# Graph layer with 16 relations: later places for the key chain, and every third tile through stage one in two fp32r parts

## The chip, the cores and the metric

One core of a Trainium2 chip runs the whole program. The metric is the device time of the execution in microseconds (us); less is better. The engines are named as the profile names them: PE is TensorE (its matmuls; PEld its weight loads), DVE is VectorE, ACT is ScalarE, POOL is GpSimd, SP is SyncE.

## The reference, cut to what matters

```python
# h: 6250 x 256, weight: 16 x 256 x 256, 206250 edges sorted by dst
transformed = einsum('ni,rio->rno', h, weight)
msg = transformed[rel_type, src] * norm          # per edge
out = segment_sum(msg, dst, num_segments=6250)   # per node
x = layernorm(x + out)
```

All of it is float32. Each edge takes the source node's row, scales it by the edge's weight `norm`, multiplies it with its relation's matrix and adds it to the row of its destination node.

## The kernel before, in words

The kernel turns the order round: it first sums the scaled source rows for each pair (node, relation) and multiplies with the matrices afterwards.

The 6250 nodes are cut into NB = 49 blocks of 128 nodes. Since the edges are sorted by destination, the edges of a block are a stretch of the edge list; the kernel takes CT = 35 tiles of 128 edges for each block, and tile t can only hit a window `WIN[t]` of the block's nodes. With 16 relations a window is 64 to 304 columns wide (column = node x 16 + relation).

**Stage one** of tile t is a matmul that scatters 128 edges: the stationary operand is the tile's gathered rows (128 edges x 128 features, for each of two feature halves h), the moving operand is `spread`, a 128-edge by window matrix that holds the edge's `norm` in the column of its key and zero elsewhere. DVE makes `spread` by comparing a column index with the edge's key and multiplying by norm (L605). The result accumulates in PSUM (`ps_a`) in four groups of 32 nodes (GROUPS = 4), two of which are open at a time (OPEN = 2); ten of the tiles touch two groups. Each float32 matmul of the program is two matmul instructions with two weight loads in the trace, so a tile in one group is four pairs (2 halves x 2), one in two groups is eight. Groups end with tiles 9, 17, 26 and 34.

A finished group is taken out of PSUM in two fp32r parts: ACT writes the upper part `a_hi` (L678), DVE the rest `a_lo` (L581). **Stage two**, one block behind, is 32 products (L766 with 512 columns, L768 with 256), all fp32r; they are dealt out over the 35 tiles of the next block's stage one, one or two after each tile from tile 4 on (`products_after`). A block's last group is taken out during tiles 3 and 4 of the next block.

**The gathers**: POOL fetches the 128 source rows of each tile with one indirect DMA (L433) into a ring of 35 slots (`rows`, ROWS = 35). Before tiles 0, 5, 10, ... it waits until PE has summed the tiles whose slots come free (`wait(pool, tiles_summed, b, CT, t + BATCH - ROWS)`). The last two tiles of a block (OPTIONAL) are only gathered when they hold edges of the block.

**The key chain** of block b + 1 runs beside the tiles of block b. Its steps stand at fixed places of the hand-written order of each engine, by the tuple PREPARE. Step 0 (ACT, tile 1) converts the loaded edge arrays `raw` to float (`convert_edges`, L658). Step 1 (PE, tile 2) transposes them into `ps_m` (`turn_edges`, L750). Step 2 (ACT, tile 4) copies them to `meta` (`copy_edges`, L666). Step 3 (DVE, tile 6) makes the indices `idx` and the keys (`keys`, L528 to L547) and signals `keys_made`, for which POOL waits before it gathers tile 0 of block b + 1. Step 4 (PE, tile 8) sums the hits of the optional tiles (`sum_hits`, L736). Step 5 (DVE, tile 12) casts that sum for POOL (`convert_hits`, L552). Block 0 has its own tuple, PREPARE_0, which is 19 more at every place.

Every engine goes through its own program in order. DVE makes `spread` at most RING = 10 tiles ahead of PE: the wait for `tiles_summed` in front of each. ACT has nothing in stage one but the evacuations, the key chain and a square root for the layer norm.

## Time and profile before

| | |
|---|---|
| median of 3 runs | 2565.3 us (2549.6 to 2580.5) |
| the profiled execution's own time | 2584.87 us |
| its span | 2583.2 us |
| mean granted TensorE clock | 0.926 |
| PE busy / POOL busy / DVE busy / ACT busy | 86% / 60% / 45% / 10% |

The profiled execution is 19.6 us above the median of the three runs. PE is the busiest engine, but its busy time is made of modelled ends of pipelined matmuls; the spacing of starts is what tells a matmul's cost. A block takes some 51 us.

### The profile page before, as it was taken

To read this page: it belongs to the slowest core of one execution; us is meant where nothing else is said; L and a number is where in the kernel's file an instruction comes from. 1 tells how busy PE (TensorE), PEld (TensorE's weight loads), DVE (VectorE), ACT (ScalarE), POOL (GpSimd) and SP (SyncE) were. 2 spreads that over 40 slices of the span, in tenths; PEclk is the share of its full clock that TensorE was granted. 3 is DMA by queue.
4 is the path that set the end of the run, shared out by engine and by line. 5 is a ranking of instruction groups with operands and counts; after the bars stand their busy time and mean duration, and the time that the engine had idled before them with its cause. 6 is when DMAs were issued, how large, how long until landed. Compare 5 with 4: busy or idle time off the path is not lost.

```text
span 2583.2 us, 33166 instructions
## 1 busy us (share of the span) xinstructions
PE 2219.3 (86%) x12267; PEld 1956.2 (76%) x12267; DVE 1151.6 (45%) x2871; ACT 271.2 (10%) x559; POOL 1560.6 (60%) x1675
## 2 busy tenths in 40 slices
PE   5589889889988998888888888888898888888888
PEld 4477777778777777777777778777787777777777
DVE  4344444344444443544444345444544444444443
ACT  2011101101111010101110011011101100110100
POOL 5666666656665666666666566666666666666660
PEclk8799999989998999999989998998999999999998
DMA  4333333333333333333333333333333333333331
GB/s 134 101 94 95 94 94 93 94 90 90 93 95 90 94 93 93 94 92 94 93 99 92 91 91 97 91 91 95 96 94 93 96 90 93 93 94 94 89 92 17
DMA packets 107084, 238.86 MB, mean 92 GB/s; under 512 B 30580, under 2 KB 54176, under 8 KB 106926
## 3 DMA queue, kind: packets, MB, share of 16 engines
q0 software_dynamic: 79056, 215.91, 29.5%
q1 hardware_dynamic: 27870, 20.81, 2.8%
q8 instruction: 103, 1.69, 0.3%
q14 instruction: 55, 0.45, 0.1%
HBM read 230.13 MB, written 6.62 MB: 92 GB/s over the span
## 4 chain that ended last, share of the span: by engine, by line
PE 77%; another core or an unknown queue 8%; issue 7%; DVE 4%; ACT 2%; SPq 0%; DMA 0%; DVEq 0%
PE ps_a L799 55%; PE ps_z L766 14%; PE ps_z L768 7%; DVE a_lo L581 2%; ACT a_hi L678 2%; DVE spread L605 1%; DMA w_raw<-in_L_gnn_weight 0%; PE ps_m L750 0%; SPq L344 0%; ACT meta L666 0%; PE ps_m L736 0%; DVE key L533 0%; DVE key_hit L542 0%; DVE hits L545 0%
## 5 line engine op out<-in xcount | busy, mean ns | idle before, releaser
L433 POOL DMA_INDIRECT rows<-in_x,idx x1646 | 1557.0, 946 | 958.5 <-issue 441.4
L799 PE MATMUL ps_a<-spread,rows 128*128 128x128 f32 (+15 forms) x8820 | 1817.3, 339 | 305.4 <-issue 174.3
L799 PEld LDWEIGHTS ps_a<-spread,rows 128*128 128x128 f32 x8820 | 1394.0, 201 | 481.4 <-issue 219.2
L766 PE MATMUL ps_z<-w_parts,a_hi 128*128 128x512 f32 x1568 | 875.3, 560 | 29.8 <-DVE a_lo L581 25.0
L605 DVE TENSOR_SCALAR spread<-ps_i,key,meta 128x272 f32<-128x272 f32 (+13 forms) x1715 | 750.7, 502 | 50.4 <-remote 29.7
L581 DVE TENSOR_TENSOR a_lo<-ps_a,a_hi 128x512 fp32r<-128x512 f32 x392 | 252.4, 686 | 1055.3 <-ACT a_hi L678 990.7
L768 PE MATMUL ps_z<-w_parts,a_lo 128*128 128x256 f32 x1568 | 453.9, 289 | 7.7 <-issue 7.7
L678 ACT ACTIVATE a_hi<-ps_a 128x512 fp32r<-128x512 f32 x392 | 212.8, 595 | 1848.9 <-PE ps_a L799 1483.5
L766 PEld LDWEIGHTS ps_z<-w_parts,a_hi 128*128 128x128 f32 x1568 | 317.1, 202 | 64.8 <-DVE a_lo L581 28.0
L768 PEld LDWEIGHTS ps_z<-w_parts,a_lo 128*128 128x128 f32 x1568 | 316.8, 202 | 37.6 <-issue 13.5
L528 DVE CAST idx<-meta 128x35 int32<-128x35 f32 x50 | 10.4, 208 | 120.7 <-ACT meta L666 117.2
L552 DVE CAST late_hits<-ps_m 1x2 int32<-1x2 f32 x49 | 7.1, 146 | 112.7 <-remote 106.1
L706 ACT ACTIVATE z_std<-z_mv,eps_col 128x1 f32<-128x1 f32 x49 | 14.4, 294 | 271.8 <-issue 204.7
L666 ACT ACTIVATE meta<-ps_m 128x140 f32<-128x140 f32 x50 | 14.6, 291 | 141.9 <-remote 138.6
L750 PE MATMUL ps_m<-ident,raw_f 35*128 35x35 f32 x150 | 18.9, 233 | 8.9 <-issue 4.8
L658 ACT ACTIVATE raw_f<-raw 35x384 f32<-35x384 int32 x50 | 25.7, 514 | 1.4 <-DMA raw<-in_edge_weight 1.4
L750 PEld LDWEIGHTS ps_m<-ident,raw_f 35*128 35x128 f32 x150 | 13.3, 139 | 16.5 <-issue 10.8
L560 DVE TENSOR_TENSOR z_own<-xr,ps_z 128x256 f32<-128x256 f32 x49 | 20.1, 411 | 9.0 <-PE ps_z L768 9.0
L564 DVE BATCH_NORM_STATS2 z_stat<-z 128x6 f32<-128x256 f32 x49 | 21.0, 428 | 1.7
L562 DVE TENSOR_TENSOR z<-z_own,ps_z 128x256 f32<-128x256 f32 x49 | 20.6, 421 | 1.7
L572 DVE TENSOR_SCALAR z_out<-z,z_mv,z_rstd 128x256 f32<-128x256 f32 x49 | 20.3, 415 | 1.8
L594 DVE TENSOR_TENSOR w_parts<-w_raw,w_parts 128x512 fp32r<-128x512 f32 x16 | 11.0, 689 | 22.2 <-issue 14.4
(52 smaller groups left out, 132.0 us busy)
## 6 DMA issues: line engine op xcount, KB each, us to landing
rows<-in_x,idx POOLq DMA_INDIRECT x1646
xr<-in_x SPq DMA_DIRECT2D x48, 128.0 KB
out<-z_out SPq DMA_DIRECT2D x48, 128.0 KB
w_raw<-in_L_gnn_weight SPq DMA_DIRECT2D x16, 256.0 KB
raw<-in_src SPq DMA_DIRECT2D x48, 17.5 KB
raw<-in_dst SPq DMA_DIRECT2D x48, 17.5 KB
raw<-in_edge_type SPq DMA_DIRECT2D x48, 17.5 KB
raw<-in_edge_weight SPq DMA_DIRECT2D x48, 17.5 KB
```

The lines of the kernel that those rows point to most:

```text
L433: pool.indirect_dma_start(rows[:, rows_slot(b, t), :], None, x, bass.IndirectOffsetOnAxis(ap=idx[:, b % 2, t:t + 1], axis=0)).then_inc(row ...
L562: dve.tensor_tensor(z[:, :], z_own[:, :], ps_z[:, b % 2, F:2 * F], ALU.add).then_inc(residual_added, 1)
L564: dve.bn_stats(z_stat[:, :], z[:, :]).then_inc(variance_steps, 1)
L572: dve.tensor_scalar(z_out[:, :], z[:, :], z_mv[:, 0:1], z_rstd[:, :], ALU.subtract, ALU.mult).then_inc(rows_normalised, 1)
L581: dve.tensor_tensor(a_lo[:, b % 2, h, :, at_g], ps_a[:, g % OPEN, h, :].rearrange("p (n r) -> p r n", r=R), a_hi[:, b % 2, h, :, at_g].bit ...
L605: dve.tensor_scalar(spread[:, slot, 0:(end - first) * R], iota[:, 0:(end - first) * R], key[:, b % 2, t:t + 1], meta[:, b % 2, 3, t:t + 1] ...
L658: act.activation(raw_f[:, :, :], raw[:, 0:3, :], ACT.Copy).then_inc(edges_converted, 1)
L678: act.activation(a_hi[:, b % 2, h, :, g * GN:(g + 1) * GN], ps_a[:, g % OPEN, h, :].rearrange("p (n r) -> p r n", r=R), ACT.Copy).then_inc ...
L750: ins = pe.transpose(ps_m[:, a * CT:(a + 1) * CT], v, ident[0:CT, 0:CT])
L766: pe.matmul(zk, a_hi[:, ak, h, r, :], w_parts[:, r, h, :, :].rearrange("p a f -> p (a f)"), start=n == 0, stop=False, skip_group_check=True)
L768: ins = pe.matmul(zk[:, 0:F], a_lo[:, ak, h, r, :], w_parts[:, r, h, 0, :], start=False, stop=n == KH * R - 1, skip_group_check=True)
L799: ins = pe.matmul(ps_a[:, g % OPEN, h, (begin - g * GN) * R:(stop - g * GN) * R], rows[:, rows_slot(b, t), h * P:(h + 1) * P], spread[:, s ...
```

## The change

It has two parts. First, three places of PREPARE move: the key chain on DVE from tile 6 to 16, the hit sum on PE from 8 to 20, the hit cast on DVE from 12 to 31. PREPARE_0 keeps its values, now written out. Second, the tiles t with t % 3 == 1 (1, 4, 7, ..., 34: twelve of 35) take another way through stage one. ACT multiplies the gathered rows by norm and rounds them to fp32r (`hi`); DVE makes a plain 0/1 matrix in fp32r (`onehot`) and the rest `lo` = rows x norm - hi; PE multiplies hi and lo, one after the other, with the same onehot, as fp32r matmuls into the same sums. The new tiles have four slots (HALVES). RING goes from 10 to 7.

```diff
-    RING = 10
+    RING = 7
+    HALVES = 4
-    PREPARE = (1, 2, 4, 6, 8, 12)
-    PREPARE_0 = tuple(t + 19 for t in PREPARE)
+    PREPARE = (1, 2, 4, 16, 20, 31)
+    PREPARE_0 = (20, 21, 23, 25, 27, 31)
+    SPLIT = tuple(t for t in range(CT) if t % 3 == 1)
+    NS = len(SPLIT)
+        def half_free(eng, b, t):
+            n = SPLIT.index(t)
+            if n >= HALVES:
+                wait(eng, tiles_summed, b, CT, SPLIT[n - HALVES] + 1)
+            else:
+                wait(eng, tiles_summed, b, CT, SPLIT[n - HALVES + NS] + 1 - CT)
 # DVE, each tile
-                        wait(dve, tiles_summed, b, CT, t + 1 - RING)
-                        dve.tensor_scalar(spread[:, slot, ...], iota[...], key[...], meta[...], is_equal, mult)
+                        if t in SPLIT:
+                            half_free(dve, b, t)
+                            dve.tensor_scalar(onehot[:, slot, 0:width], iota[:, 0:width], key[:, b % 2, t:t + 1],
+                                              None, ALU.is_equal).then_inc(split_parts_made, 1)
+                            wait(dve, upper_made, b, NS, SPLIT.index(t) + 1)
+                            dve.scalar_tensor_tensor(out=lo[:, slot, :], in0=rows[:, rows_slot(b, t), :],
+                                                     scalar=meta[:, b % 2, 3, t:t + 1],
+                                                     in1=hi[:, slot, :].bitcast(F32), op0=ALU.mult,
+                                                     op1=ALU.subtract).then_inc(split_parts_made, 1)
+                        else:
+                            (as before, with RING = 7)
 # ACT, each tile, behind the key chain's steps and ahead of the evacuations
+                        if t in SPLIT:
+                            (wait for the gathered rows of t)
+                            half_free(act, b, t)
+                            act.activation(hi[:, half_slot(t), :], rows[:, rows_slot(b, t), :], ACT.Copy,
+                                           scale=meta[:, b % 2, 3, t:t + 1]).then_inc(upper_made, 1)
 # PE, each tile
+                        if split:
+                            wait(pe, split_parts_made, b, 2 * NS, 2 * SPLIT.index(t) + 2)
+                            parts, cols = (hi[:, half_slot(t), :], lo[:, half_slot(t), :]), onehot[...]
...
-                            for g in groups:
-                                ins = pe.matmul(ps_a[...], rows[..., h * P:(h + 1) * P], spread[...], ...)
+                            for m, part in enumerate(parts):
+                                for g in groups:
+                                    ins = pe.matmul(ps_a[...], part[:, h * P:(h + 1) * P], cols[...], ...)
```

The waits of `copy_edges` count the split tiles apart from the others; nothing else changes.

## Rows read from the trace of the kernel before

**Rows 1.** The page: busy time by engine, and the chain that ended last.

```profile
PE 2219.3 (86%) x12267; PEld 1956.2 (76%) x12267; DVE 1151.6 (45%) x2871; ACT 271.2 (10%) x559; POOL 1560.6 (60%) x1675
...
PE 77%; another core or an unknown queue 8%; issue 7%; DVE 4%; ACT 2%; SPq 0%; DMA 0%; DVEq 0%
```

**Rows 2.** Waits: who waited for whom, us in total, times, longest.

```profile
PE ps_a L799 <- issue: 174.3, 238, 10.6
...
PE ps_a L799 <- DVE spread L605: 126.8, 43, 6.1
DVE idx L528 <- ACT meta L666: 117.2, 22, 6.6
...
POOL rows L433 <- DVEq L536: 75.3, 22, 11.3
```

**Rows 3.** Timeline of all engines: two steps of the key chain and what follows.

```profile
306.92 0.37 PE L750 MATMUL ps_m<-ident,raw_f 35*128 35x35 f32 x3
...
312.83 0.29 ACT L666 ACTIVATE meta<-ps_m 128x140 f32<-128x140 f32 x1 [6.01 <-remote]
...
315.14 0.96 PE L799 MATMUL ps_a<-spread,rows 128*128 128x176 f32 x4 [4.37 <-DVE spread L605]
...
1342.82 0.19 PE L736 MATMUL ps_m<-key_hit,ones 128*1 128x2 f32 x2
...
1349.27 0.15 DVE L552 CAST late_hits<-ps_m 1x2 int32<-1x2 f32 x1 [4.53 <-remote]
```

**Rows 4.** Timeline of POOL, the first and last of ten gathers, then the next.

```profile
1364.68 0.94 POOL L433 DMA_INDIRECT rows<-in_x,idx  x1 [1.49 <-PE ps_a L799]
...
1375.92 0.95 POOL L433 DMA_INDIRECT rows<-in_x,idx  x1 [0.30 <-issue]
1379.53 0.94 POOL L433 DMA_INDIRECT rows<-in_x,idx  x1 [2.66 <-PE ps_a L799]
```

**Rows 5.** Timeline of POOL, the first and last of 25 gathers, then the next.

```profile
64.08 0.94 POOL L433 DMA_INDIRECT rows<-in_x,idx  x1 [11.32 <-DVEq L536]
...
94.08 0.95 POOL L433 DMA_INDIRECT rows<-in_x,idx  x1 [0.30 <-issue]
99.38 0.94 POOL L433 DMA_INDIRECT rows<-in_x,idx  x1 [4.36 <-remote]
```

**Rows 6.** Windows: busy time, clock, DMA share, GB/s in two stretches.

```profile
74.00:100.00 26.00, 6.04 (x29) 4.91 (x29) 4.12 (x11) 0.00 (x0) 16.69 (x18) 0.62 0.35 97
1350.00:1400.00 50.00, 43.14 (x240) 38.27 (x239) 23.30 (x59) 4.93 (x11) 31.97 (x34) 0.90 0.31 90
```

**Rows 7.** Timeline of PE, 1325 to 1332 us: start, us, operation.

```profile
1325.31 1.19 PE L799 MATMUL ps_a<-spread,rows 128*128 128x304 f32 x4
...
1326.68 1.19 PE L799 MATMUL ps_a<-spread,rows 128*128 128x304 f32 x4
...
1329.21 0.81 PE L799 MATMUL ps_a<-spread,rows 128*128 128x192 f32 x4
...
1330.21 0.61 PE L799 MATMUL ps_a<-spread,rows 128*128 128x128 f32 x4
...
1331.00 0.55 PE L799 MATMUL ps_a<-spread,rows 128*128 128x64 f32 x4
```

**Rows 8.** Groups by line, weight loads: busy, mean ns of one, idle before.

```profile
L799 PEld LDWEIGHTS ps_a<-spread,rows 128*128 128x128 f32 x8820 | 1394.0, 201 | 481.4 <-issue 219.2 <-DVE spread L605 144.0
L766 PEld LDWEIGHTS ps_z<-w_parts,a_hi 128*128 128x128 f32 x1568 | 317.1, 202 | 64.8 <-DVE a_lo L581 28.0 <-issue 8.7
```

**Rows 9.** Groups by line, shapes apart: the nearest operations to the added ones.

```profile
L678 ACT ACTIVATE a_hi<-ps_a 128x512 fp32r<-128x512 f32 x392 | 212.8, 595 | 1848.9 <-PE ps_a L799 1483.5 <-remote 250.2 <-issue 115.2
...
L562 DVE TENSOR_TENSOR z<-z_own,ps_z 128x256 f32<-128x256 f32 x49 | 20.6, 421 | 1.7
```

**Rows 10.** Timeline of DVE in one block: the keys, and tile 15's spread.

```profile
1338.10 0.23 DVE L528 CAST idx<-meta 128x35 int32<-128x35 f32 x1
...
1351.83 1.41 DVE L605 TENSOR_SCALAR spread<-ps_i,key,meta 128x240 f32<-128x240 f32 x3
```

More of the change, by code:

```diff
@@ L114, in build @@
     OPTIONAL = (CT - 2, CT - 1)
+    SPLIT = tuple(t for t in range(CT) if t % 3 == 1)
+    NS = len(SPLIT)
+    assert NS % HALVES == 0 and CT % ROWS == 0
     CONFIRM = 3
@@ L189, in build @@
         rows = sb("rows", [P, ROWS, F])
+        hi = sb("hi", [P, HALVES, F], F32R)
+        lo = sb("lo", [P, HALVES, F], F32R)
+        onehot = sb("onehot", [P, HALVES, WMAX], F32R)
         spread = sb("spread", [P, RING, WMAX])
@@ L602, in tile_block @@
                         first, end = WIN[t]
-                        wait(dve, tiles_summed, b, CT, t + 1 - RING)
-                        dve.tensor_scalar(spread[:, slot, 0:(end - first) * R], iota[:, 0:(end - first) * R],
-                                          key[:, b % 2, t:t + 1], meta[:, b % 2, 3, t:t + 1],
-                                          ALU.is_equal, ALU.mult).then_inc(spreads_made, 1)
+                        width = (end - first) * R
+                        if t in SPLIT:
+                            half_free(dve, b, t)
+                            slot = half_slot(t)
+                            dve.tensor_scalar(onehot[:, slot, 0:width], iota[:, 0:width], key[:, b % 2, t:t + 1],
[6 more added lines that the diff above has]
+                        else:
+                            wait(dve, tiles_summed, b, CT, t + 1 - RING)
+                            dve.tensor_scalar(spread[:, ring_slot(b, t), 0:width], iota[:, 0:width],
+                                              key[:, b % 2, t:t + 1], meta[:, b % 2, 3, t:t + 1],
+                                              ALU.is_equal, ALU.mult).then_inc(spreads_made, 1)
                     for g in range(GROUPS):
@@ L783, in tile_block @@
                             seek_turn()
-                        wait(pe, spreads_made, b, CT, t + 1)
-                        if t in OPTIONAL:
-                            wait(pe, optional_rows_in, b, 1, 1)
-                        else:
-                            wait(pe, rows_in[t], b, 16, 16)
+                        split = t in SPLIT
+                        if split:
+                            wait(pe, split_parts_made, b, 2 * NS, 2 * SPLIT.index(t) + 2)
+                            parts, cols = (hi[:, half_slot(t), :], lo[:, half_slot(t), :]), onehot[:, half_slot(t), :]
+                        else:
+                            wait(pe, spreads_made, b, CT - NS, sum(n not in SPLIT for n in range(t + 1)))
+                            if t in OPTIONAL:
+                                wait(pe, optional_rows_in, b, 1, 1)
+                            else:
+                                wait(pe, rows_in[t], b, 16, 16)
+                            parts, cols = (rows[:, rows_slot(b, t), :],), spread[:, ring_slot(b, t), :]
                         first, end = WIN[t]
@@ L796, in tile_block @@
                                     wait(pe, a_lower_made, b, GROUPS * KH, KH * (g - OPEN) + h + 1)
-                            for g in groups:
-                                begin, stop = max(first, g * GN), min(end, (g + 1) * GN)
-                                ins = pe.matmul(
-                                    ps_a[:, g % OPEN, h, (begin - g * GN) * R:(stop - g * GN) * R],
-                                    rows[:, rows_slot(b, t), h * P:(h + 1) * P],
-                                    spread[:, slot, (begin - first) * R:(stop - first) * R],
-                                    start=group_tiles[g][0] == t, stop=False, skip_group_check=True)
+                            for m, part in enumerate(parts):
+                                for g in groups:
+                                    begin, stop = max(first, g * GN), min(end, (g + 1) * GN)
+                                    ins = pe.matmul(
+                                        ps_a[:, g % OPEN, h, (begin - g * GN) * R:(stop - g * GN) * R],
+                                        part[:, h * P:(h + 1) * P],
+                                        cols[:, (begin - first) * R:(stop - first) * R],
+                                        start=group_tiles[g][0] == t and m == 0, stop=False, skip_group_check=True)
                         ins.then_inc(tiles_summed, 1)
```

15 lines of the change are left out of this document (12 added, 3 removed).

## The prediction, made before the changed kernel was run

> **What bounds the kernel now.** I read the page first: its chain that ended last is 77% PE, and PE is busy 86% of the span [rows 1]. Busy time alone would say that less matmul work is less time. The waits correct that: besides its work PE loses 174.3 us with nothing that the profile can name and 126.8 us waiting for DVE's spreads, DVE waits 117.2 us in its key step for ACT's meta, and POOL waits 75.3 us for the keys [rows 2]. So I looked at the places where this happens. PE's transposes of the next block start at 306.92 and take 0.37 us, but ACT, which waits for nothing else, copies their result only at 312.83; DVE has to wait with its keys, and PE with the next spread, until 315.14 after an idle 4.37 us. In another block the hit sum starts at 1342.82 and DVE casts it at 1349.27, 6.5 us later [rows 3]. The signal of a matmul that is long done comes 5 to 6 us late.
>
> When it is late can be read on POOL. A gather starts every 1.25 us ((94.08 - 64.08) / 24 [rows 5]) while nothing stops it. At 1364.68 POOL begins ten in a row, the last at 1375.92, and then sits 2.66 us until PE's slots are reported free at 1379.53 [rows 4]. The late signals lie inside such unbroken runs, and come through some two microseconds after the run ends. Ten is the longest run of the steady state. The warm-up has one of 25, from 64.08 to 94.08, and POOL goes on at 99.38 [rows 5]. In its stretch from 74 to 100 us PE is busy 6.04 us of 26, at a mean granted clock of 0.62; in an ordinary stretch it is busy 43.14 of 50, at 0.90 [rows 6]. So a long run does to PE what a short one does not: PE can work ahead of its own late signals for a few tiles, no more. I take as this kernel's second bound that the gathers must come in runs of at most about ten. They need 33 to 35 x 1.25 = 41 to 44 us of a block's 51 us, and the 7 to 10 us that are left are the pauses that let PE's signals through.
>
> **Split tiles, PE.** Two neighbouring tiles of 304 columns start 1.37 us apart, a tile of 192 and its successor 1.00 us [rows 7]; both stretches hold four matmuls and one product. The difference over 4 x 112 columns is 0.83 ns a column, two cycles at 2.4 GHz, and what is left, 0.36 us, is the product: 512 + 256 fp32r columns at 0.47 ns, so about one cycle a column at 512 and 256. The tiles of 128 and 64 columns are 0.79 us apart, which makes 0.11 us a matmul at either width, a floor [rows 7]. The split keeps the number of matmuls (four a group) and takes one cycle a column in place of two. Per tile, 4 x (0.83 x width ns, at least 110) less 4 x (0.42 x width, at least 110): nothing for tiles 1, 16 and 34, 0.10 for tile 4, 0.04 for 7, 0.31 for 10, 0.36 each for 13 and 31, 0.41 for 19, 0.45 for 22, 0.20 for 25, 0.51 for 28. That is 2.75 us a block, 49 blocks: -135 us. No fp32r matmul under 256 columns is in this trace. The bounds: one cycle there too (the nearest rows, of the same type), or no better than float32's four cycles over its two matmuls, which paid twice by hi and lo is +4.1 us a block, +200 us. I take one cycle, the rate of the type's own rows; the split at 256 and more alone gives 1.37 us a block.
>
> The Trainium skill ("TensorE: Matmul & The Clock Gate", Weight-path perf modes) says that weight loads go up to four times as fast when the type is not FP32. If fp32r counted as another type, the floor would fall for the parts and the saving would rise to an estimated 5.0 us a block. The trace has the weight loads of both types at 201 and 202 ns [rows 8], so I leave it a small chance.
>
> **Split tiles, the other engines.** DVE's onehot has the shape of the spread that it replaces: nothing. `lo` is new: 12 times, as DVE's 128x256 two-operand add, 421 ns [rows 9], 5 us a block on an engine that is busy 45%. `hi` on ACT is half the elements of the evacuation's 595 ns [rows 9], between 0.3 and 0.6 us, 12 times, 4 to 7 us on an engine busy 10%. Both are beside PE's work. But the order matters: `hi` of tile 4 stands on ACT behind the meta copy, which waits for PE's transposes of tile 2. Before, only the key chain waited there; now `hi`, `lo`, and PE's tile 4 do. With a prompt signal that is 0.3 + 0.45 + 0.42 us of chain against 1.1 us of PE's tiles 2 and 3, next to nothing; with a late one it is the whole 5.9 us [rows 3]. I take 1.5 us a block, bounds 0 and 5.7: +70 us. RING 7 leaves DVE seven tiles ahead, 7 x 1.2 us = 8 us, more than a late signal: nothing, at most 1 us a block where the tiles are short.
>
> **The key chain's places.** DVE no longer waits for meta at tile 6. That returns at most the 126.8 us that PE waited for spreads [rows 2]; I take -100. The hit sum at 20 and the cast at 31 carry two small operations and a wait each; POOL needs the cast only before its tile 33, after the block's end. Nothing.
>
> What the key step also moves is the gathers. POOL may not gather tile 0 of the next block before `keys_made`. In one block the keys start at 1338.10; the place ahead of tile 16 is right after tile 15's spread, at 1351.83 + 0.5 [rows 10]. So the next block's gathers start 14 us later, while PE is in its tile 11 or 12. Today POOL stands at its slot limit nearly always, and each batch of five is let through by PE's next five tiles: that makes the pauses. After the change POOL is idle from the end of one block's gathers (42 us after they began) to the next keys, some 9 us at one stretch: all of the slack in one place, in which nothing is held up. When it starts, PE has done 11 tiles, so ten gathers are free at once; the batches at 10 and 15 need 15 and 20 tiles, and PE has them, since its signals are late only from about the fifth gather on, at tile 15 or 16. The first run is then 15 to 20 long. Price: in the run of 25 PE did 6.04 us of work in the 26 us that followed its first eight gathers [rows 6], so about 1 to 1.25 us are lost for each gather beyond ten. I take 15: +6.25 us a block, bounds 0 (the gate shuts at ten as now) and 12.5 (a run of 20). The keys move for 47 blocks (block 0 keeps its places): +294 us.
>
> The clock follows the stalls: 0.90 in the ordinary stretch, 0.62 in the starved one [rows 6]. If the mean goes from 0.926 to 0.88, the 37 us of PE work in a block take 2 us more: +94 us, bounds 0 and 190.
>
> **The sum** is -135 + 70 - 100 + 294 + 94 = +223 us on the profiled execution's own 2585, 2808. The median of the runs is 20 us lower: **2790 us**. With the bounds of the run's length and of the clock it goes from 2650 to 2950.
>
> **The rivals.**
> - The longer run does no harm, or does not come about: POOL is stopped at ten by the late signals themselves, as now. For it speaks that it is a feedback (a slower PE closes the gate sooner), and that both long runs of the trace are in the warm-up, where PE lacked products and keys too. Against it, PE has ample work in the stretch of rows 6. Then the split's 135 us and a part of the key wait remain: 2565 - 135 = 2430, from 2380 to 2480 by what of the 100 the wait at tile 4 takes back.
> - Narrow fp32r matmuls cost as much as float32's or twice that: this ends on the slow side without any gathers. It decides where a part is under 256 columns, in twelve of the fifteen tile-and-group pairs. With the forecast's gathers 2790 + 67 = 2857 up to 2790 + 334 = 3124; with harmless gathers up to 2765.
> - Gains and losses cancel: a run only two gathers longer (+2.5 us a block) eats the split and the key wait: 2540 to 2590.
> - The weight loads of the parts are faster, by the skill's rule above: the saving is 5.0 in place of 2.75 us a block, 110 us less, 2680 with the forecast's gathers. The rows speak against it.
>
> **How the numbers follow.** Forecast 0.45, harmless gathers 0.26, narrow parts dear 0.17, cancelling 0.09, faster weight loads 0.03. Faster by over 1% is the second alone, 0.26; within 1% (about what a measurement of this kernel tells from no change) the fourth, 0.09; slower the rest, 0.65. The forecast's own range is 2650 to 2950. The range that should hold the time 8 times in 10 has to take in the fast side: 2425 to 2960 leaves out half of the second case and of the third, some 0.17.
>
> **What the profile of the changed kernel would show.** Right: gathers in runs of 15 and more once a block, after a wait for the keys of some 9 us; PE idle with no named cause growing from 174 us to several hundred; the granted clock under 0.90; DVE's wait for meta gone from the keys, and PE waiting for `lo` of tile 4. Wrong: runs of ten at most, and a block under 50 us. The rates can be read from the starts of tiles 28 (304 columns) and 31 (240): 0.87 and 0.80 us to the next tile for one cycle a column, if tile 31 takes 1.16 us it is no faster than before, and with 1.96 us it is twice as dear. What would make the whole wrong is the reading that the runs cause the late signals: if it is the other way round, POOL's pause being the effect of a signal that is late for another reason, then the place of the keys costs nothing.

## The result, and the profile after

| | before | after |
|---|---|---|
| median | 2567.7 us (4 runs) | 3028.9 us (4 runs, 3006.5 to 3033.8) |
| the profiled execution's own time | 2584.87 us | 3029.99 us |
| mean granted TensorE clock | 0.926 | 0.809 |

The ratio is 1.1785, 95% interval 1.1692 to 1.1878: 461 us slower. The ratios here and below leave out the three executions that ran more slowly than the fastest of their own kernel by over 1.5%; without its one, the median of "changed, lo of one operand" is 2982 us in place of 2995. The page of the changed kernel, busy times and chain (to be held against [rows 1]):

```profile
PE 2317.6 (77%) x12267; PEld 2029.8 (67%) x12267; DVE 1359.4 (45%) x3459; ACT 507.7 (17%) x1147; POOL 1577.0 (52%) x1675
...
PE 66%; issue 20%; another core or an unknown queue 7%; DVE 5%; ACT 2%; DMA 0%; POOL 0%; SPq 0%; ACTq 0%; DVEq 0%
```

"issue", time for which the profile names no cause, was 7% of the chain and is 20%. The waits of the changed kernel (who for whom, us in total, times, longest) answer to [rows 2]:

```profile
POOL rows L453 <- PE ps_a L851: 721.3, 98, 18.7
DVE lo L631 <- ACT hi L738: 626.7, 119, 30.8
DVE spread L637 <- remote: 611.6, 130, 9.2
...
PE ps_a L851 <- issue: 428.7, 340, 4.0
...
PE ps_z L811 <- issue: 142.8, 100, 2.4
...
PE ps_a L851 <- DVE lo L631: 58.6, 4, 30.1
```

PE's idle time without a named cause on the rows of the two main operations is 428.7 + 142.8 us, in place of 174.3 on the one such row of before. Not all of it is without a cause. The row that names `lo` has only 58.6 us, all in the warm-up, but a wait for several signals can be booked as "issue". In one block:

```profile
1335.15 0.29 ACT L699 ACTIVATE meta<-ps_m 128x140 f32<-128x140 f32 x1 [4.42 <-remote]
1335.86 0.48 DVE L631 SCALAR_TENSOR_TENSOR lo<-rows,meta,hi 128x256 fp32r<-128x256 f32 x1 [7.99 <-ACT hi L738]
1336.40 0.50 PE L851 MATMUL ps_a<-onehot,hi 128*128 128x160 f32 x1 [3.94 <-issue]
```

PE's transposes end at 1331.2, ACT copies meta 4 us later, then come `hi` and `lo` of tile 4, and PE starts tile 4 at 1336.40, 0.06 us after `lo` has ended. The kernel has PE wait for that `lo`. After the warm-up PE stands so before tile 4 in 45 blocks, 129 us together; with the warm-up 192 us of PE's idle time end within 0.15 us of the end of a `lo`. DVE's key step no longer waits for meta, and PE's wait for spreads falls from 126.8 to 16.0 us. POOL's timeline in one block: the first and the last gather of a run, and what comes after it.

```profile
1287.80 0.94 POOL L453 DMA_INDIRECT rows<-in_x,idx  x1 [10.96 <-PE ps_a L851]
...
1311.83 0.95 POOL L453 DMA_INDIRECT rows<-in_x,idx  x1 [0.30 <-issue]
1316.71 0.94 POOL L453 DMA_INDIRECT rows<-in_x,idx  x1 [3.93 <-remote]
...
1349.20 0.94 POOL L453 DMA_INDIRECT rows<-in_x,idx  x1 [12.96 <-PE ps_a L851]
```

(1311.83 - 1287.80) / 1.25 + 1 = 20 gathers in a row, after 10.96 us of idle time. The wait is put down to PE, but it is the key step that ends it: the keys of the next block stand at 1348.32 on DVE, right ahead of the gather at 1349.20. Runs of 20 come in 46 of 48 blocks; the wait in front of them has a median of 13.0 us. PE's timeline during that run:

```profile
1301.35 0.39 PE L851 MATMUL ps_a<-spread,rows 128*128 128x208 f32 x2 [0.86 <-issue]
1302.06 0.22 PE L851 MATMUL ps_a<-spread,rows 128*128 128x64 f32 x1 [0.32 <-issue]
1303.47 0.48 PE L811 MATMUL ps_z<-w_parts,a_hi 128*128 128x512 f32 x1 [1.20 <-issue]
...
1306.29 0.84 PE L851 MATMUL ps_a<-spread,rows 128*128 128x160 f32 x2 [0.98 <-issue]
1308.39 0.37 PE L851 MATMUL ps_a<-spread,rows 128*128 128x128 f32 x1 [1.25 <-issue]
...
1312.61 0.37 PE L851 MATMUL ps_a<-spread,rows 128*128 128x128 f32 x1 [0.35 <-issue]
1315.41 0.59 PE L811 MATMUL ps_z<-w_parts,a_hi 128*128 128x512 f32 x1 [2.43 <-issue]
```

From the eleventh gather on PE issues an instruction every 0.7 to 2.8 us, and recovers some 3 us after the run's last gather. Some of these gaps lie between matmuls of one tile, for which the kernel has PE wait for nothing. The rates of the split tiles, from the same timeline later in the block:

```profile
1322.84 0.30 PE L851 MATMUL ps_a<-onehot,hi 128*128 128x304 f32 x1
...
1323.75 1.19 PE L851 MATMUL ps_a<-spread,rows 128*128 128x304 f32 x4
...
1326.49 0.27 PE L851 MATMUL ps_a<-onehot,hi 128*128 128x240 f32 x1
...
1327.28 0.48 PE L851 MATMUL ps_a<-spread,rows 128*128 128x192 f32 x2
```

Tile 28 takes 0.91 us to its successor (1.37 before) and tile 31 takes 0.79: narrow fp32r matmuls are as cheap as the forecast took them (0.87 and 0.80).

### The profile page after: what moved, and what is told of

The parts are those of the page before. It is cut to its first block, busy times and chain, and to the rows that moved or that the text cites. A ratio compares the mean times of both kernels' runs of the same rounds, so it can differ in the third digit from the quotient of the medians.

```text
span 3028.3 us, 34387 instructions
## 1 busy us (share of the span) xinstructions
PE 2317.6 (77%) x12267; PEld 2029.8 (67%) x12267; DVE 1359.4 (45%) x3459; ACT 507.7 (17%) x1147; POOL 1577.0 (52%) x1675
## 4 chain that ended last, share of the span: by engine, by line
PE 66%; issue 20%; another core or an unknown queue 7%; DVE 5%; ACT 2%; DMA 0%; POOL 0%; SPq 0%; ACTq 0%; DVEq 0%
PE ps_a L851 45%; PE ps_z L811 14%; PE ps_z L813 7%; DVE a_lo L601 2%; DVE spread L637 1%; DVE lo L631 1%; ACT a_hi L711 1%; ACT hi L738 1%; DVE onehot L627 0%; POOL rows L453 0%; PE ps_m L795 0%; PE ps_m L781 0%; DMA w_raw<-in_L_gnn_weight 0%; DMA rows<-in_x,idx 0%
## 5 line engine op out<-in xcount | busy, mean ns | idle before, releaser
L851 PE MATMUL ps_a<-spread,rows 128*128 128x176 f32 (+16 forms) x5880 | 1364.2, 361 | 312.3 <-issue 290.0
L851 PEld LDWEIGHTS ps_a<-spread,rows 128*128 128x128 f32 x5880 | 1025.5, 216 | 455.2 <-issue 348.7
L811 PE MATMUL ps_z<-w_parts,a_hi 128*128 128x512 f32 x1568 | 856.7, 547 | 150.3 <-issue 142.8
L637 DVE TENSOR_SCALAR spread<-ps_i,key,meta 128x288 f32<-128x288 f32 (+12 forms) x1127 | 539.2, 507 | 693.9 <-remote 611.6
L631 DVE SCALAR_TENSOR_TENSOR lo<-rows,meta,hi 128x256 fp32r<-128x256 f32 x588 | 280.7, 477 | 800.8 <-ACT hi L738 626.7
L851 PE MATMUL ps_a<-onehot,hi 128*128 128x128 f32 (+10 forms) x1470 | 374.5, 300 | 198.8 <-issue 138.6
L851 PEld LDWEIGHTS ps_a<-onehot,hi 128*128 128x128 f32 x1470 | 293.3, 215 | 244.2 <-issue 163.9
L851 PE MATMUL ps_a<-onehot,lo 128*128 128x128 f32 (+10 forms) x1470 | 377.8, 305 | 0.0
L851 PEld LDWEIGHTS ps_a<-onehot,lo 128*128 128x128 f32 x1470 | 292.0, 218 | 1.9 <-issue 1.8
L738 ACT ACTIVATE hi<-rows,meta 128x256 fp32r<-128x256 f32 x588 | 264.9, 502 | 12.1 <-DMA rows<-in_x,idx 11.0
L627 DVE TENSOR_SCALAR onehot<-ps_i,key 128x240 fp32r<-128x240 f32 (+4 forms) x588 | 256.3, 436 | 0.0
L751 ACT ACTIVATE z_std<-z_mv,eps_col 128x1 f32<-128x1 f32 x49 | 14.4, 295 | 265.1 <-DVE z_mv L586 259.6
L699 ACT ACTIVATE meta<-ps_m 128x140 f32<-128x140 f32 x50 | 14.4, 287 | 172.2 <-remote 149.7
```

The source lines that it names most:

```text
L627: dve.tensor_scalar(onehot[:, slot, 0:width], iota[:, 0:width], key[:, b % 2, t:t + 1], None, ALU.is_equal).then_inc(split_parts_made, 1)
L631: dve.scalar_tensor_tensor(out=lo[:, slot, :], in0=rows[:, rows_slot(b, t), :], scalar=meta[:, b % 2, 3, t:t + 1], in1=hi[:, slot, :].bitc ...
L637: dve.tensor_scalar(spread[:, ring_slot(b, t), 0:width], iota[:, 0:width], key[:, b % 2, t:t + 1], meta[:, b % 2, 3, t:t + 1], ALU.is_equa ...
L738: act.activation(hi[:, half_slot(t), :], rows[:, rows_slot(b, t), :], ACT.Copy, scale=meta[:, b % 2, 3, t:t + 1]).then_inc(upper_made, 1)
L811: pe.matmul(zk, a_hi[:, ak, h, r, :], w_parts[:, r, h, :, :].rearrange("p a f -> p (a f)"), start=n == 0, stop=False, skip_group_check=True)
L851: ins = pe.matmul(ps_a[:, g % OPEN, h, (begin - g * GN) * R:(stop - g * GN) * R], part[:, h * P:(h + 1) * P], cols[:, (begin - first) * R: ...
```

## Experiments

**All runs.** Kernels with the same chip in the table were measured together, with the kernel before beside them. It turned out that the chips are of two kinds. On some the kernel before takes 2098 to 2104 us, here called prompt chips (P1 to P3); on others 2561 to 2606, here called late chips (L1 to L3), and the measurement above is of that kind. Times are compared on one chip; between chips only ratios are compared. "Keys at 16 only" leaves out the split but moves all three steps of the key chain, the two hit steps too.

| kernel | chip | us | before | ratio (95%) |
|---|---|---|---|---|
| split, keys at 6 | P1 | 2117.5 | 2098.3 | 1.0094 (1.0077 to 1.0111) |
| keys at 16 only | P1 | 2098.6 | 2098.3 | 0.9999 (0.9989 to 1.0008) |
| hit steps only | P1 | 2099.2 | 2098.3 | 1.0003 (0.9993 to 1.0012) |
| changed, lead 25 | P1 | 2112.6 | 2098.3 | 1.0069 (1.0052 to 1.0085) |
| changed | P2 | 2114.1 | 2099.6 | 1.0067 (1.0050 to 1.0084) |
| changed, pauses | P2 | 2476.2 | 2099.6 | 1.1793 (1.1773 to 1.1812) |
| before, half the gathers | L1 | 2082.6 | 2561.4 | 0.8134 (0.8080 to 0.8188) |
| changed, half the gathers | L1 | 2007.3 | 2561.4 | 0.7827 (0.7778 to 0.7876) |
| changed, lo of one operand | L1 | 2994.8 | 2561.4 | 1.1670 (1.1550 to 1.1790) |
| keys at 16 only | L2 | 2837.9 | 2605.4 | 1.0935 (1.0846 to 1.1023) |
| split, keys at 6 | L2 | 2612.5 | 2605.4 | 1.0023 (0.9978 to 1.0068) |
| changed, pauses | L2 | 2679.3 | 2605.4 | 1.0328 (1.0243 to 1.0413) |
| before, paced 128 | P3 | 2291.5 | 2103.6 | 1.0892 (1.0874 to 1.0910) |
| keys at 16, RING 7 | P3 | 2103.8 | 2103.6 | 1.0001 (0.9992 to 1.0011) |
| changed, keys at 15 | P3 | 2118.7 | 2103.6 | 1.0069 (1.0052 to 1.0086) |
| changed, keys at 12 | P3 | 2108.6 | 2103.6 | 1.0025 (1.0016 to 1.0035) |
| before, paced 288 | L3 | 2523.5 | 2606.2 | 0.9690 (0.9638 to 0.9742) |
| changed, keys at 15 | L3 | 2883.1 | 2606.2 | 1.1074 (1.1015 to 1.1133) |

### One part alone, on P1

```diff
 # split, keys at 6 (the changed kernel)
-    PREPARE = (1, 2, 4, 16, 20, 31)
+    PREPARE = (1, 2, 4, 6, 8, 12)
 # keys at 16 only (the kernel before)
-    PREPARE = (1, 2, 4, 6, 8, 12)
+    PREPARE = (1, 2, 4, 16, 20, 31)
 # hit steps only (the kernel before)
-    PREPARE = (1, 2, 4, 6, 8, 12)
+    PREPARE = (1, 2, 4, 6, 20, 31)
 # changed, lead 25: the gathers may lead PE by fewer tiles
-                        wait(pool, tiles_summed, b, CT, t + BATCH - ROWS)
+                        wait(pool, tiles_summed, b, CT, t + BATCH - 25)
```

> The changed kernel with PREPARE back at (1, 2, 4, 6, 8, 12): the split stays, with RING 7. Gather-run theory (the keys' late place makes POOL issue 20 gathers without a pause, and PE starves in them): runs of at most 10 again, 2420 to 2570 us, most likely 2480, a little under the kernel before for the cheaper matmuls (-135 at most). Split theory (the hi/lo chain through ACT and DVE and RING 7 cost the time): it stays above 2850. If each carries a half: about 2750.

> The kernel before with PREPARE = (1, 2, 4, 16, 20, 31) alone: no split, RING 10. Gather-run theory: runs of 15 to 20 in every block and a granted clock near 0.8, 2950 to 3080 us, at or above the changed kernel, which has the cheaper matmuls. Split theory: 2540 to 2600, as the kernel before or a little faster, since DVE's wait for meta is gone.

> The kernel before with only the hit sum at tile 20 and the hit cast at tile 31; the keys stay at tile 6. Gather-run theory: these two have nothing to do with it, 2540 to 2590 us. Rival (it is the hit steps' waits that stop PE and POOL): above 2650.

> The changed kernel, keys at 16, but POOL may lead PE by 25 tiles at most and not by 35 (only the constant in its wait for tiles_summed changes; the same gathers in the same order). Gather-run theory: when the keys come no 20 gathers are allowed any more, runs of 5 to 10, 2450 to 2620 us. Rival (the keys' late place costs by something else: the idle POOL, late rows, DVE's order): 2900 to 3100, or more, since the rows come later still.

No expectation was met, of either theory: the kernel before itself was 470 us faster than where it had been measured. Two of these kernels never ran on a late chip. One moves the hit steps alone, so their share of the loss there is not separated from that of the keys. The other lets the gathers lead PE by only 25 tiles, with the keys still at 16; it would have been the direct trial of the run's length. The page of the hit-steps kernel, whose time is that of the kernel before:

```profile
PE 2040.7 (97%) x12267; PEld 1832.3 (87%) x12267; DVE 1146.1 (55%) x2871; ACT 274.3 (13%) x559; POOL 1562.8 (75%) x1675
...
PE 67%; POOL 19%; issue 7%; DMA 6%; DVE 0%; ACT 0%; POOLq 0%; SPq 0%; DVEq 0%
```

After the fifth, its gathers never wait for longer than 0.84 us, and PE is 97% busy. In the stretch from 74 to 100 us, where the prediction read the price of a long run off PE's 6.04 busy us [rows 6], PE is busy 25.14 us here at a granted clock of 1.00:

```profile
74.00:100.00 26.00, 25.14 (x143) 21.89 (x141) 11.30 (x26) 2.57 (x5) 19.60 (x22) 1.00 0.36 105
```

So a long run of gathers does not starve PE on this chip. ACT's meta copy waits for PE's transposes 50 times, 29.0 us in all and never over 1.1 us; in the kernel before, as first measured, the same wait is put down to a remote signal and is up to 7.5 us long. The two rows, of P1 and of the first measurement:

```profile
ACT meta L666 <- PE ps_m L750: 29.0, 50, 1.1
```

```profile
ACT meta L666 <- remote: 138.6, 22, 7.5
```

The signals themselves can be read from the trace's record of semaphore steps. What PE reports at the end of a tile, on a late chip (the kernel before, in the run of [rows 4]) and on P1 (hit steps only):

```
late chip: PE ends a tile at   1373.08 1374.40 1375.77 1377.14 1378.51
           steps of its signal 1375.47 | 1379.04 1379.12 1379.19 1379.27 1379.34
P1:        PE ends a tile at   1301.63 1302.90 1304.16
           steps of its signal 1301.65 1302.91 1304.17
```

On P1 a step follows within 0.02 us. On the late chip four tiles and more go unreported while the gathers' own steps arrive (16 for each gather on P1, of which the late chip's record shows 2 to 5 here), and then come out in a row, 0.07 to 0.08 us apart, once the run is over. The record on the late chip is itself incomplete, with 1496 steps for 1715 tiles, so it shows the delay but not each step. That the reports stand in a queue behind the gathers' is how I read it; no run looks into it.

### The changed kernel itself again, and with pauses

The first has no edit; the second (P2, and again on L2) has, ahead of every fifth gather:

```diff
                         wait(pool, tiles_summed, b, CT, t + BATCH - ROWS)
+                        for n in range(2):
+                            wait(pool, paused, b, 2 * CT // BATCH, 2 * t // BATCH + n)
+                            pool.memset(pause[:, :], 0.0).then_inc(paused, 1)   # 128 x 512
```

> The changed kernel itself, unedited, beside the kernel before on the same chip. The occasion theory (what made PE's signals late is a property of the chip or occasion of the first measurement, not of a long run of gathers): where the kernel before takes 2098 us, as in the first four experiments, the changed kernel takes 2110 to 2125 us, as its two relatives did, at a clock of 0.98; where the kernel before takes about 2565, the changed one takes 3000 to 3040 again. The run theory (the keys at 16 concentrate POOL's gathers into runs of 20 and more, and these starve PE): it is at least 10% above the kernel before on any chip, 2300 us or more.

> The changed kernel with a pause of about 1.1 us on POOL ahead of every fifth gather (two small memsets of a scratch tensor, one after the other), so that no run of gathers is longer than five. Where POOL is the bound (the kernel before at 2098 us): 7 x 1.1 x 49 = 377 us more, about 2490. Where PE's signals are late (the kernel before at 2565 us): the run theory expects the pauses to let the signals through, 2500 to 2650 in place of 3029; the rate theory (what counts is the share of time in which POOL gathers, not the length of a run) expects little change, 2950 to 3050.

The changed kernel costs 0.7% on P2, as expected for such a chip, and 17.9% on the first chip. That the change starves PE by its runs is no property of the kernel alone. The pauses cost 362 us where POOL is the bound (377 expected). The chain of the changed kernel on P2 shows that bound:

```profile
POOL 46%; PE 24%; issue 17%; DMA 6%; DVE 5%; ACT 1%; POOLq 1%; SPq 0%; ACTq 0%; DVEq 0%
```

### Half the gathers, and lo of one operand, on L1

```diff
 # half the gathers: after block 0 the odd tiles (but the optional ones) are not gathered
-                    else:
+                    elif t % 2 == 0:
                         gather(b, t)
 # and PE (and ACT) wait for such a tile only in block 0
-                            wait(pe, rows_in[t], b, 16, 16)
+                            wait(pe, rows_in[t], 0 if t % 2 else b, 16, 16)
 # lo of one operand (the changed kernel)
-                            dve.scalar_tensor_tensor(out=lo[...], in0=rows[...], scalar=meta[...],
-                                                     in1=hi[...], op0=ALU.mult, op1=ALU.subtract)
+                            dve.tensor_scalar(lo[...], rows[...], meta[...], 0.0, ALU.mult, ALU.mult)
```

> The kernel before with every second gather of blocks 1 to 48 left out (the odd tiles but the optional ones use the rows that block 0 left in their slots, so the sums are not the reference's). Gathers no longer bound it. Where the full kernel takes 2098 us: if POOL's 1646 gathers of 1.25 us set its time, the tiles' median spacing of 41 us a block is what is left and the time is 2030 to 2060; if PE sets it already, 2090 to 2100. Where the full kernel takes 2565 us with PE's signals late: 2050 to 2150 if the gathers make them late, 2500 or more if something else does.

> The changed kernel with the same gathers left out. The prediction's term for the split tiles is 2.75 us a block of PE time, 135 us: with the gathers out of the way it should be 135 us (110 to 150) below the other kernel of this kind, about 1910, if hi and lo come in time. If the parts of the split arrive late (their chain over ACT and DVE is the bound) it is within 40 us of it. If narrow fp32r matmuls were no cheaper, it is equal or slower.

> The changed kernel with lo made from rows and the scalar alone, one SBUF operand in place of two (lo is then zero, so the parts do not add up to the rows). In the changed kernel gathers that overlap a lo take 1072 ns in place of 947, and the mean gather is 956 ns against 947.6, 1646 times 8.6 ns = 14 us, the whole of its 15 us over the kernel before. If the second SBUF operand is what holds POOL up: 2098 to 2102, gathers back at 947 ns. If any DVE operation that reads rows from SBUF does it: 2110 to 2120 as before; if the one-operand form in its fast mode holds it more: above 2125.

Half the gathers bring the kernel before from 2561 to 2083 us on a late chip, below what it takes whole on a prompt one; its meta copies wait as on P1:

```profile
ACT meta L666 <- PE ps_m L750: 29.1, 49, 1.4
```

So it is the gathers that make the signals late there. The split is worth 75 us with them out of the way (2082.6 to 2007.3), not 135; this lies between what the two theories had expected (110 to 150, or within 40). PE's busy time falls by 103 us (2025.8 to 1922.8). The third kernel met a late chip, so the expected 2098 us could not be tried; its gathers can be read all the same. What the gathers cost in each kernel (group of POOL's indirect DMA: busy, mean ns), the hit-steps kernel, the changed kernel on P2 and the one with lo of one operand:

```profile
L433 POOL DMA_INDIRECT rows<-in_x,idx x1646 | 1559.5, 947 | 504.9 <-issue 463.6 <-PE ps_a L799 37.8 <-DVEq L536 3.2
```

```profile
L453 POOL DMA_INDIRECT rows<-in_x,idx x1646 | 1573.9, 956 | 504.9 <-issue 478.2 <-PE ps_a L851 22.8 <-DVEq L556 3.2
```

```profile
L453 POOL DMA_INDIRECT rows<-in_x,idx x1646 | 1565.3, 951 | 1358.3 <-PE ps_a L849 785.0 <-issue 451.4 <-remote 81.4
```

The idle time on both prompt chips is the same 504.9 us; the busy time is 14.4 us more, and the changed kernel is 14.5 us slower. In the hit-steps kernel 16 gathers are longer than 0.96 us, in the changed one 110, of which 99 lie beside a `lo` (958 gathers do in all). One of them, on P2 (POOL, then DVE):

```profile
1300.14 1.18 POOL L453 DMA_INDIRECT rows<-in_x,idx  x1 [0.30 <-issue]
```

```profile
1300.03 0.48 DVE L631 SCALAR_TENSOR_TENSOR lo<-rows,meta,hi 128x256 fp32r<-128x256 f32 x1
```

On the late chips 134 of 324 gathers beside a `lo` are long in the changed kernel, 44 of 357 with lo of one operand: the second operand is most of it, not all. That the 14.5 us on a prompt chip go away with it was not tried. The Trainium skill ("SBUF — State Buffer", Who interferes with whom) says that a VectorE instruction with two SBUF inputs contends with a GpSimd one that reads SBUF; this agrees. Why the rate with one operand is still nearly a third of the other, no run here explains.

The third kernel's time says something on the runs too. It is at 1.1670, close to the changed kernel's 1.1785, but its gathers come in runs of 15 in 39 blocks and of 20 in only 8. By the pattern of runs in a block (all from this one trace, from the first gather of a block to that of the next):

```
runs in the block     blocks   us a block   POOL's idle time after the first run
20, 5, 8 or 9         8        62.6         4.0
15, 5, 5, 8 or 9      22       61.1         1.6
15, 10, 8 or 9        13       56.7         3.0
```

So a run of 15 that is broken off for only 1.6 us costs nearly as much as one of 20. The length of the run by itself is not the price.

### The two parts and the pauses, on L2

The same three kernels as above, now on a late chip.

> The kernel before with the key chain at 16, hit sum at 20, hit cast at 31, no split tile: the same text as the earlier keys-only run, now wanted on a chip where PE's signals are late (the kernel before at 2561 us; if the chip is one of those where it takes 2098, all three of this call only repeat what is known: 2098, 2117, 2476). Run theory, as predicted: gathers in runs of 15 and more, 200 to 400 us slower, 2760 to 2950. Split theory (the waits of hi and lo behind late signals are what costs): 2540 to 2590.

> The changed kernel with the key chain, hit sum and hit cast back at 6, 8 and 12. With the kernel before at 2561 us: run theory: gathers in runs of at most 10 again, the split's gain is left, 75 to 135 us less a wait at tile 4, 2430 to 2520. Split theory: most of the loss stays, 2850 to 3000.

> The changed kernel with a pause of about 1.1 us on POOL ahead of every fifth gather. With the kernel before at 2561 us and the changed one near 3000: if signals pile up only while gathers follow each other without a pause, the pauses that add 377 us of POOL's time take 400 to 500 us off: 2480 to 2600. If the number of gathers in a block's time counts and not their runs, 2900 to 3050.

The moved keys alone cost 9.4%, in the range expected by the run theory; the split alone costs nothing, which neither theory had: 2612 us against 2430 to 2520 or 2850 to 3000, with the kernel before at 2605 and not 2561. Waits of the keys-only kernel, and POOL in one of its blocks:

```profile
POOL rows L433 <- DVEq L536: 481.6, 49, 25.1
...
PE ps_a L799 <- issue: 290.8, 308, 2.6
```

```profile
1367.04 0.94 POOL L433 DMA_INDIRECT rows<-in_x,idx  x1 [8.96 <-DVEq L536]
...
1384.54 0.95 POOL L433 DMA_INDIRECT rows<-in_x,idx  x1 [0.30 <-issue]
1388.62 0.94 POOL L433 DMA_INDIRECT rows<-in_x,idx  x1 [3.13 <-remote]
```

After 9 us of waiting for the keys come (1384.54 - 1367.04) / 1.25 + 1 = 15 gathers, in 47 blocks. The split with keys at 6 has no run over ten in its steady state and loses its gain to another wait, that of PE for `lo`. Its row has 217.6 us; with what the profile books as "issue" 281 us of PE's idle time end within 0.15 us of a `lo`:

```profile
PE ps_a L851 <- DVE lo L631: 217.6, 74, 28.2
```

With pauses the changed kernel is 3.3% over the kernel before in place of 17.9%, though they add 362 us to POOL's work: breaking the runs gives back far more than it costs. It stays 79 us above the upper end expected. But the pauses do not let the signals through: the copy of meta comes 7.0 us (median) after PE's transposes, the longest of all kernels here. What ends is the starving of PE: its idle time booked as "issue", the waits for `lo` taken out, is 113 us against 476 in the changed kernel, while those waits grow from 192 to 330.

### Spacing in place of pauses, and the keys one tile earlier, on P3 and L3

```diff
 # paced 128 and paced 288 (the kernel before): a memset of so many columns behind every gather
                     else:
                         gather(b, t)
+                    wait(pool, paused, b, CT, t)
+                    pool.memset(pause[:, :], 0.0).then_inc(paused, 1)
 # keys at 16 only, RING 7
-    RING = 10
+    RING = 7
 # changed, keys at 15 (or 12)
-    PREPARE = (1, 2, 4, 16, 20, 31)
+    PREPARE = (1, 2, 4, 15, 20, 31)
```

> The kernel before with one small memset on POOL (128 columns, 0.2 us) behind every gather, so that gathers come at best every 1.45 to 1.5 us. Backlog theory: on the slow chips a gather's signals take about 1.47 us to go through (after runs of 5, 10 and 20 gathers POOL's pauses are 1.1 to 1.2, 2.3 and 3.6 us, 0.23 to 0.18 us for each gather), and whatever is signalled meanwhile waits behind them. Then with this spacing nothing piles up: on a chip where the kernel before takes 2565 to 2605, 2440 to 2520, and almost the same time (2420 to 2500, 1715 times 0.2 to 0.25 us more than 2098) on a chip where it takes 2098. If spacing does not matter and only the count of gathers does: 2600 or more on the slow chip.

> The kernel before with the moved key chain and RING 7 in place of 10, no split tile. On the slow chips, keys at 16 alone gave 47 runs of 15 gathers (first gather with 12 tiles of the block done) and 2838 us; the changed kernel 46 runs of 20 (13 tiles done) and 3029. If the shorter ring is why the run grew from 15 to 20: runs of 20, 2950 to 3050. If the split's own waits are: runs of 15, 2830 to 2850.

> The changed kernel with the key chain one tile earlier, at 15. Run theory: if the first gather then finds 12 tiles done in place of 13, the gate shuts at 15, and 5 gathers fewer in the run are 5 x 1.0 to 1.25 us x 47 = 235 to 294 us less: 2740 to 2800. If DVE reaches both places at the same moment (it stands at tile 14 for the evacuation of group 0): as the changed kernel, 2990 to 3040. On a chip where the kernel before takes 2098: 2114 like its relatives.

> The changed kernel with the key chain at 12, ahead of DVE's wait for the evacuation at tile 14. Run theory: first gather with 7 to 10 tiles done, runs of 10, a time near that of the changed kernel with keys at 6 (2613): 2560 to 2680. If it is the split with late signals that costs and the keys' place little: 2900 or more.

> The kernel before with a memset of 288 columns behind every gather in place of 128, so that gathers come every 1.47 us (they came every 1.34 us with 128). Backlog theory, on a chip where the kernel before takes 2565 to 2605: no backlog builds up, late signals all but vanish, and the time is that of POOL's spacing, 1646 x 1.47 + 60 = 2480, range 2450 to 2530. If the spacing does not matter: above 2600. On a chip where the kernel before takes 2098 to 2104: 2480 to 2510.

> The changed kernel with the key chain at 15, the same text as the earlier one. On a chip where the kernel before takes 2565 to 2605: if the first gather then finds 12 tiles done in place of 13 and the gate shuts at 15, 2740 to 2800; if DVE reaches both places at the same moment, 13 tiles, runs of 20, 2990 to 3040. On a chip where the kernel before takes 2098 to 2104: 2119 again.

On P3 the four say little on the question. The pace came out at 1.34 us, not 1.45, so the time is 2291 us and not 2420. The ring of 7 and the keys at 16 cost nothing there; on a late chip the ring was not tried. Keys at 12 leave 53 long gathers in place of 112 with keys at 15, and 5 us in place of 15, though nearly as many lie beside a `lo` (911 and 924): overlap alone does not decide.

On L3, one tile earlier, the first gather finds 12 tiles done where it found 13, the gate of the fourth batch shuts, and the run is 15 long in 47 blocks; the ratio falls from 1.1785 to 1.1074. The run came out as the run theory had it, the time did not: 2883 us against 2740 to 2800. PE now stands 347 us for `lo` in place of 192, which that expectation left out. A table from the gathers' and tiles' times (medians), with the delay from the end of PE's transposes to ACT's copy. The tiles are those that PE has done of a block when POOL gathers tile 0 of the next; on a prompt chip POOL gets there 29 tiles on, long after keys made at 16, so their place does not matter:

```
kernel, chip                  tiles done at   run that    delay of the
                              first gather    starts      meta copy, median us
before, first chip            6               5 (to 10)   3.86
split, keys at 6, L2          5               5 (to 10)   3.43
keys at 16 only, L2           12              15          6.22
changed, keys at 15, L3       12              15          4.18
changed, first chip           13              20          2.55
lo of one operand, L1         13              15 (to 20)  3.90
changed, pauses, L2           15              5           7.04
half the gathers, L1          5               3           0.04
hit steps only, P1            29              endless     0.04
before, paced 288, L3         6 to 33         33, 34      2.50
```

The paced kernel is 3.1% faster than the kernel before on L3, in the range expected, with series of 33 and 34 gathers 1.47 us apart. But its delay is still 2.5 us, and over 1 us in 30 of 48 blocks: that the late signals all but vanish was wrong. No kernel here beats both on both kinds of chip: pacing at 1.34 us already costs 8.9% on P3, 2291 us where 2420 to 2500 had been expected.

## Why the prediction was wrong in size

PE's time in the two traces (page and idle rows) can be held against the terms of the sum, in us:

```
                                        before   changed   difference   forecast
PE busy (split and clock together)      2219.3   2317.6    +98          -135 + 94 = -41
idle, ends with a lo                    0        192       +192         +70
idle, ends with a spread                127      16        -111         -100
idle, "issue" without those             194      476       +282         +294
the rest                                43       26        -17          0
span                                    2583.2   3028.3    +445         +223
```

- **The sign and the mechanism.** "All of the slack in one place", a wait for the keys, then an unbroken run, then PE starved: seen in 46 or 47 of 48 blocks. It is caused by the moved steps: they alone cost 9.4% on L2, and one tile less of the move gave time back on L3. This was the likeliest case and it came. The wait for the keys was some 9 us with the keys alone and 13 in the changed kernel.
- **The step that failed first is the length of the run: "I take 15: +6.25 us a block".** It was 20, the other end of the bound, in the changed kernel; it is 15 with the keys alone. By the ratios the way from the keys at 15 to the keys at 16 is worth some 175 us (1.1074 to 1.1785, on two late chips; the two intervals alone allow some 25 us either way). That these are the price of five more gathers is not shown: with `lo` of one operand the first run is mostly 15 and the ratio is 1.1670.
- **The terms that were too small are the wait at tile 4 and the clock.** The term of the runs, +294, looks right beside the measured +282, but by luck. Ten gathers beyond the tenth lost 0.6 us each, where five had been taken at 1.25. What the sum misses in the trace lies elsewhere: the chain meta, `hi`, `lo` in front of tile 4 was taken at 1.5 us a block, +70, and took 192 us (2.9 us in each of 45 blocks, the rest nearly all in the warm-up). PE's work was to fall by 41 us and grew by 98.
- **The clock, +94.** It fell to 0.809, not 0.88; with the keys alone, runs of 15, to 0.894, with keys at 15 to 0.857. PE's busy time rose by 98 us although the split takes 74 us off it between the two prompt chips (2040.7 to 1966.2) and 103 with half the gathers. An estimate from these: the lower clock cost 170 to 200 us. It comes with the stalls, and no run holds it still.
- **Why 20.** The prediction had PE at "tile 11 or 12" when the keys are made. It was 12 with the keys alone and 13 in the changed kernel. In both, DVE stands at its tile 14 for the evacuation of group 0, which needs PE's tile 9, and the first gather comes 3.20 us (median) after the end of tile 9; the prediction named no such queue. In that time PE, with cheaper split tiles, does one tile more. But 13 tiles do not make a run of 20. Its fourth batch needs the report of tile 20. That tile ends 7.9 us after the first gather both in the changed kernel and with `lo` of one operand, some 11 us ahead of the gate; in the one the gate is open in 45 of 46 blocks, in the other, on another late chip, in 8 of 46. The report is in by then in one case and mostly not in the other, and why stays open.
- **The bound was found and not carried.** 12.5 us a block in place of 6.25 makes 2808 + 294 = 3102 us; the text ended its range at 2950. A range with its own bound in it would have held 3029, which also lies beyond the wide range of 2425 to 2960.
- **The split, -135.** The rate was right (tiles 28 and 31 above). The gain is 75 us where nothing else is late, and nothing on a late chip with all gathers, because PE then stands 281 us for `lo` in place of the 70 taken, as much as the upper bound (5.7 us a block is 279).
- **The key wait, -100.** This came: PE's wait for spreads fell by 111 us. With the keys alone it stayed (121.9 us), so the split tiles have a part in it.
- **The faster weight loads.** The parts' loads take 215 and 218 ns and float32's 216 in the changed kernel, so the rule of the Trainium skill ("TensorE: Matmul & The Clock Gate", Weight-path perf modes) does not show for fp32r:

```profile
L851 PEld LDWEIGHTS ps_a<-spread,rows 128*128 128x128 f32 x5880 | 1025.5, 216 | 455.2 <-issue 348.7 <-DVE spread L637 11.8
...
L851 PEld LDWEIGHTS ps_a<-onehot,hi 128*128 128x128 f32 x1470 | 293.3, 215 | 244.2 <-issue 163.9 <-DVE lo L631 59.9
```

- **"The runs cause the late signals"**, the reading on which the whole was said to rest, is false on prompt chips. On late ones the gathers make the signals late (with half of them the delay is gone), but not the length of the runs alone: with pauses every five gathers it is 7.0 us. The long unbroken runs go with the starving of PE. The one trace of before could not tell that. Why a chip is of one kind or the other stays open.

## What to carry to other kernels

When a step that releases a queue of work is moved, work out how far its consumers and producers have got at the moment of release, all waits ahead of it on its engine counted, and how much of the queue is then free at once: the gate here counts in fives, and one place of the key step went with 1.11 in place of 1.18. Carry every bound of the dearest term to the range. Where a new operand comes through a chain that starts at a late signal, take the lateness as its price, 2.5 to 6 us here, and not a fraction of it. When a profile books a stall as "issue", look at what ended just before it. And measure a kernel with many indirect DMAs on more than one chip, since one and the same pair differed by 0.7% on one and by 18% on another.

## What the runs showed of the hardware

- The kernel before takes 2098 to 2104 us on three chips and 2561 to 2606 on others. In place of 0.04 us, a signal of PE takes 2.5 to 7.0 us (medians) on the latter while POOL gathers 128 rows every 1.25 us, with or without pauses of 1.3 us after every five; with every second gather left out it takes 0.04 us there too.
- On late chips POOL's idle time after a run grows with the run: 1.5 us after 5 gathers and 2.6 after 10 (kernel before), 3.1 after 15 (keys at 16 only), 3.9 after 20 (changed), where 0.3 lie between any two gathers. It is 2.8 after the run of 5 that follows one of 20. That would fit a queue that drains; at a spacing of 1.47 us the delay is still 2.5 us.
- PE's own instructions come 0.7 to 2.8 us apart in the second half of a run of 20, with nothing named that they wait for.
- A gather whose time overlaps a VectorE operation with two SBUF operands takes up to 0.3 us longer (on P2, 99 of the 958 that overlap; the 1646 gathers take 14 us more in all). Where gathers are the bound this is as much as the whole cost of the change there, 14.5 us.
